# Attention: float16 maxima, one product per group, a new slot table, and the causal mask added by TensorE

## The reference, cut to what matters

```
scores = einsum('bhqd,bhkd->bhqk', q, k)        # 256 queries, 256 keys, per batch and head
scores = where(causal, scores, -inf)            # only in the self-attention of the third block
weights = softmax(scores, axis=-1)
out = einsum('bhqk,bhkd->bhqd', weights, v)
```

## Time and profile before

| | |
|---|---|
| Median of 3 runs | 3341.56 us (3337.22 to 3347.16) |
| The profiled execution, its own time | 3335.4 us |
| Its span, first to last instruction | 3333.7 us |
| Mean granted TensorE clock | 0.895 |
| PE busy | 2558.5 us (77%) |
| DVE busy | 2258.7 us (68%) |
| ACT busy | 1245.9 us (37%) |
| POOL busy | 924.7 us (28%) |

### The profile page before, as it was taken

The page is one execution under the profiler, slowest core; times in us unless marked ns, Lnnn a source line. Parts: engine busy times, 40 slices in busy tenths (PEclk is TensorE's granted clock), DMA queues, the critical chain, the costliest instruction groups (busy, mean ns, idle before and its releaser), DMA issues. The chain is left out here.

```text
span 3333.7 us, 58668 instructions
## 1 busy us (share of the span) xinstructions
PE 2558.5 (77%) x21348; PEld 1660.5 (50%) x21348; DVE 2258.7 (68%) x5909; ACT 1245.9 (37%) x2228; POOL 924.7 (28%) x1324
## 2 busy tenths in 40 slices
PE   2997367999424367997989776996799999869962
PEld 1443355666323135886456543443565555546651
DVE  5997745666467434666677777997666555777768
ACT  1886334333122103111346564772322222226611
POOL 3442460100350520112655325871000000024200
PEclk9998689999757678999989987998799999889986
DMA  4330454222322215665631012100100000011001
GB/s 111 114 130 30 161 203 154 76 76 77 114 80 80 76 39 181 221 226 192 215 101 52 17 48 93 47 22 5 61 9 12 1 1 1 6 38 46 21 8 56
DMA packets 158163, 266.84 MB, mean 80 GB/s; under 512 B 22635, under 2 KB 106137, under 8 KB 151876
## 3 DMA queue, kind: packets, MB, share of 16 engines
q1 hardware_dynamic: 131204, 186.97, 16.9%
q0 software_dynamic: 17904, 76.23, 6.8%
q10 hardware_dynamic: 8784, 0.04, 0.2%
HBM read 175.25 MB, written 88.34 MB: 79 GB/s over the span
## 5 line engine op out<-in xcount | busy, mean ns | idle before, releaser
L1380 ACT ACTIVATE l2e_hf<-l2e_H 128x512 f32<-128x512 f32 x208 | 124.2, 597 | 375.9 <-PE l2e_H L1336 375.9
L1416 DVE CAST l2e_hh<-l2e_hf 128x512 f16<-128x512 f32 x208 | 88.7, 427 | 127.1 <-ACT l2e_hf L1380 112.0
L688 DVE TENSOR_REDUCE l0a_mx<-l0a_S 128x2 f32<-128x512 f32 x256 | 164.3, 682 | 11.9 <-PE l0a_S L530 11.2
L1336 PE MATMUL l2e_H<-l2o_hi,l2e_w 128*128 128x512 f16 x576 | 151.8, 382 | 14.9 <-DVE l2e_w L1392 14.9
L637 ACT ACTIVATE l0a_pf<-l0a_ST 128x512 f32<-128x512 f32 x256 | 145.9, 598 | 40.5 <-PE l0a_ST L544 34.8
L228 POOL TENSOR_TENSOR l3in_n_rstd<-l3in_n_sq,all_mhalf 128x8 f32<-128x8 f32 x4 | 6.9, 1724 | 553.8 <-DVE l3in_n_sq L152 553.8
L1336 PE MATMUL l2e_H<-l2e_hh,l2e_w 128*128 128x512 f16 x640 | 155.1, 379 | 0.0
L684 DVE CUSTOM_DVE_ANT_0 l2s_masked<-l2s_S,l2s_mq 128x128 f32<-128x128 f32 (+1 forms) x512 | 150.7, 349 | 6.1 <-PE l2s_S L530 5.7
L1380 ACT ACTIVATE l0e_hf<-l0e_H 128x512 f32<-128x512 f32 x128 | 76.4, 597 | 206.7 <-PE l0e_H L1336 206.7
L1336 PE MATMUL l1e_H<-l1b_hi,l1e_w 128*128 128x256 f16 (+1 forms) x936 | 145.4, 275 | 7.8 <-DMA l1e_w<-packed,all_second_weight_row 7.8
L1418 DVE TENSOR_TENSOR l2e_hl<-l2e_hf,l2e_hh 128x512 f16<-128x512 f32 x208 | 144.0, 692 | 7.2
(11 more groups left out here) (726 smaller groups left out, 7448.6 us busy)
## 6 DMA issues: line engine op xcount, KB each, us to landing
l0e_wf<-in_L_ffn_w SPq DMA_DIRECT2D x16, 1024.0 KB, 7.2
rows<-l0a_zeros SPq DMA_DIRECT2D x16, 640.0 KB, 6.1
l1u_rb<-rows SPq DMA_DIRECT2D x20, 512.0 KB, 4.7
results<-l1e_y SPq DMA_DIRECT2D x39, 256.0 KB, 3.9
l0a_kv<-in_ctx SPq DMA_DIRECT2D x16, 512.0 KB, 4.3
rows<-l0a_zeros SPq DMA_DIRECT2D x16, 512.0 KB
l0d_p_cx<-in_ctx SPq DMA_DIRECT2D x16, 512.0 KB, 5.8
l0u_rb<-rows SPq DMA_DIRECT2D x16, 512.0 KB, 5.7
```

Of the source, the lines that this page charges most:

```text
L688: m = nc.vector.tensor_reduce(mx[h % 2][:, :, i], ps[:, :].rearrange("p (u k) -> p u k", u=TB), AX.X, ALU.max)
L1336: mm = pe.matmul(bank[0:fn, :], W[par][0:kn, at + k * wd + f0:at + k * wd + f0 + fn], X, start=(done == 0), stop=(done == k_all - 1))
L1380: nc.scalar.activation(hf[q % 4][0:fn, :], pair_of(q, lay)[0][0:fn, :], lay.func, scale=1.0 / WS).then_inc(acted, 1)
L1416: nc.vector.tensor_copy(high, v).then_inc(hi_done, 1)
```

## The change

It has five parts.

1. **Maxima in float16.** `mx` becomes float16, `bound` and `nm` are gone, and `turn_max` turns `mx` itself with the float16 identity. `copy_max` then copies float16 rows.
2. **One product per group in `divide`.** The two multiplications of 128x128 become one of 128x256; `on` gets another order of its elements, and GpSimd's `add` reads it accordingly.
3. **New slots.** With 16 heads `turn_max` moves from slot 1 to 2, `copy_max` and its DMAs from 3 to 4, `divide` from 4 to 3, and `turn` is split: queries at slot 5, keys at slot 7, both before at 4. With 8 heads `turn_back` moves from slot 2 to 1, `turn_max` from 0 to 1, `copy_max` from 1 to 2, `turn` from 2 to 3.
4. **Causal stage.** After each of the two `scoreT` products of a head TensorE adds the mask to the diagonal square: a product of the bfloat16 identity with `late` (0, or -2^100 where the key is later than the query), all 128 rows, 128 columns, into the same `ST`. `weigh` waits for `probs`.
5. `cut_late` is gone; GpSimd makes `late` and `ident_b` once, at the start of the stage.

```diff
-    BACK_AT, MAX_AT, TURN_AT = (1, 1, 4) if heads == 16 else (2, 0, 2)
-    COPY_AT, DIV_AT, KEYS_AT, SUM_AT = (3, 4, 1, 5) if heads == 16 else (1, 3, 1, 3)
+    BACK_AT, MAX_AT, TURN_Q_AT, TURN_K_AT = (1, 2, 5, 7) if heads == 16 else (1, 1, 3, 3)
+    COPY_AT, DIV_AT, KEYS_AT, SUM_AT = (4, 3, 1, 5) if heads == 16 else (2, 3, 1, 3)
...
-        mx = [st.sb(f"mx{i}", [P, TB, HALF]) for i in range(2)]
-        nm = [st.sb(f"nm{i}", [P, TB, HALF]) for i in range(2)]
+        mx = [st.sb(f"mx{i}", [P, TB, HALF], F16) for i in range(2)]
...
-                def cut_late(n):
-                    t = pf[n % NPF][:, 0:2 * S].rearrange("p (u q) -> p u q", u=TB)[:, :, 0:P]
-                    pool.wait_ge(probs, n + 1)
-                    nc.gpsimd.affine_select(out=t, in_=t, compare_op=ALU.is_ge, fill=0.0, base=0,
-                                            pattern=[[0, TB], [1, P]], channel_multiplier=-1).then_inc(cut, 1)
+                def make_late():
+                    nc.gpsimd.memset(late[:, :], 0.0).then_inc(late_set, 1)
+                    nc.gpsimd.tensor_copy(ident_b[:, :], g.ident[:, :]).then_inc(late_set, 1)
+                    pool.wait_ge(late_set, 2)
+                    nc.gpsimd.affine_select(out=late[:, :], in_=late[:, :], compare_op=ALU.is_ge, fill=NEG,
+                                            base=0, pattern=[[1, P]], channel_multiplier=-1
+                                            ).then_inc(late_set, 1)
...
                     m = pe.matmul(ST_ps[n % 2][:, t_at[u]:t_at[u] + S - query_from[u]],
                                   kT[h % RING][r0:r0 + rows, j, u * P:u * P + P],
-                                  qT[h % RING][r0:r0 + rows, j, query_from[u]:S], start=True, stop=True)
+                                  qT[h % RING][r0:r0 + rows, j, query_from[u]:S], start=True, stop=not causal)
+                    if causal:
+                        if n == 0:
+                            pe.wait_ge(late_set, 3)
+                        m = pe.matmul(ST_ps[n % 2][:, t_at[u]:t_at[u] + P], ident_b[:, :], late[:, :],
+                                      start=False, stop=True)
...
-                        pe.wait_ge(cut if causal else probs, (w + 1) * G)
+                        pe.wait_ge(probs, (w + 1) * G)
...
                 def turn_max(h):
-                    pe.wait_ge(nm_set, h + 1)
+                    pe.wait_ge(maxed, (h + 1) * HALF)
                     pe.wait_ge(q_turned, min(h + 3, NH))
                     for u in range(TB):
-                        m = pe.transpose(N_ps[0:HALF, u, :], nm[h % 2][:, u, :], g.ident[:, :])
+                        m = pe.transpose(N_ps[0:HALF, u, :], mx[h % 2][:, u, :], ident_h[:, :])
                     m.then_inc(nm_turned, 1)
...
-                def bound(h):
-                    dve.wait_ge(maxed, (h + 1) * HALF)
-                    if h >= 2:
-                        dve.wait_ge(nm_turned, h - 1)
-                    nc.vector.tensor_scalar(nm[h % 2][:, :, :], mx[h % 2][:, :, :], -NEG_H, NEG_H, ALU.min, ALU.max
-                                            ).then_inc(nm_set, 1)
```

More of the change, by code:

```diff
@@ L362, in attention_stage @@
         rs = st.sb("rs", [P, 2 * TB, G])
-        on = [st.sb(f"on{i}", [P, TB, P]) for i in range(2)]
+        on = [st.sb(f"on{i}", [P, 2, TB, P // 2]) for i in range(2)]
         ident_h = st.sb("ident_h", [P, P], F16)
@@ L513, in _ @@
                             make_mask()
+                            make_late()
                     if i == HALF - 1 and out_res is None and 0 <= j - 4 < NH:
@@ L565, in weigh, with turn, turn_queries @@
                         m.then_inc(weighed, 1)
-                def turn(h):
+                def turn(h, i):
+                    v = (qs, ks)[i][h // 2 % 2][:, :, :, :].rearrange("p t h r -> p t (h r)")
+                    for c in range(4):
+                        for u in range(TB):
+                            j = h % 2 * 4 + c
+                            m = pe.transpose(MH_ps[i][:, c * TB + u, :], v[:, u, j * P:j * P + P], ident_h[:, :])
+                    m.then_inc(chunks, 1)
+                def turn_queries(h):
                     b = h // 2
@@ L615, in _ @@
                         turn_max(j - 1)
-                    if i == TURN_AT and 0 <= j + 2 < NH:
-                        turn(j + 2)
+                    if i == TURN_Q_AT and 0 <= j + 2 < NH:
+                        turn_queries(j + 2)
+                    if i == TURN_K_AT and 0 <= j + 2 < NH:
+                        turn_keys(j + 2)
             @block.scalar
@@ L715, in divide @@
                         dve.wait_ge(o_done, h - 1)
-                    for u in range(TB):
-                        if out_res is None:
-                            dst = on[h % 2][:, u, :]
-                        else:
-                            dst = out_res[:, b * TB + u, h % 2 * P:h % 2 * P + P]
-                        m = nc.vector.tensor_tensor(
-                            dst.rearrange("p (s g d) -> p s g d", s=2, d=dh), sums[:, u:2 * TB:TB, :, 0:dh],
-                            rs[:, u:2 * TB:TB, :].unsqueeze(3).to_broadcast([P, 2, G, dh]), ALU.mult)
-                    m.then_inc(o_mul, 1)
+                    if out_res is None:
+                        dst = on[h % 2][:, :, :, :].rearrange("p s u (g d) -> p (s u) g d", d=dh)
+                    else:
+                        dst = out_res[:, b * TB:(b + 1) * TB, h % 2 * P:h % 2 * P + P].rearrange(
+                            "p u (s g d) -> p s u g d", s=2, d=dh)
+                        sums = sums.rearrange("p (s u) g e -> p s u g e", s=2)
+                    by = rs[:, :, :] if out_res is None else rs[:, :, :].rearrange("p (s u) g -> p s u g", s=2)
+                    nc.vector.tensor_tensor(
+                        dst, sums[..., 0:dh], by.unsqueeze(len(by.shape)).to_broadcast(list(by.shape) + [dh]),
+                        ALU.mult).then_inc(o_mul, 1)
                 for j, i, n in slots():
-                    if i == 0 and 0 <= j - 1 < NH:
-                        bound(j - 1)
                     if i == 0 and 0 <= j + 1 < NH:
```

26 lines of the change are left out of this document (11 added, 15 removed).

## The result

The changed kernel takes 3446.12 us (median of 4 runs, 3437.21 to 3464.36) against 3342.38 of the kernel before, a ratio of 1.0317 [1.0292, 1.0342]. That is +104 us where +76 was forecast: slower, as predicted, and 8 us above the upper end of the range. The profiled execution took 3439.64 us, span 3437.9, mean granted clock 0.888.

The account below looks back on a forecast made before the run. TensorE bounds the 8-head stages, VectorE l2s, both are near 89% busy in l0a; with masks TensorE bounds l2s. Causal +85, 8-head -16, l0a +7 make +76 on 3335.4, 3411, put at 3414 us; range 3362 to 3438.

Parts of the forecast that it names:

- The causal stage: In l2s, masks make TensorE set the round at 9.05 us, +2.6 us per round, +85 us in all.
- a switch, 0.09 us: On TensorE, each change of the array's form between products loses 0.09 us; a causal slot becomes 0.70 us.
- The weigh run ahead of `turn_max`: In the l2s round, two weigh runs are counted at 0.57 us each with a change of form behind them.
- half the switches: Rival for l2s: only the way back from each mask costs 0.09; stage +40 us, total about 3370; chance 0.10.
- the masks ride along: Rival for l2s: masks cost only their columns, round 6.5 us, total about 3308, faster; chance 0.06.
- The clock: Rival: l2s falls to 1.2 GHz, columns per round double, +150 us, total 3560; chance 0.03.
- The sum: All attention stages: +85 - 16 + 7 = +76 us on 3335.4 gives 3411 us; forecast put at 3414.
- The 8-head stages: l2a and l3a, bound by TensorE: round 5.75 to 5.46 us, -8 us per stage, -16 us together.
- The wait of 0.19 behind the weigh run: In l2a, turn_max waits 0.19 us for copy_queries; in slot 1 this wait goes.
- two float16 blocks instead of two float32 ones: turn_max gets cheaper, from 0.21 to 0.11 us, saving 0.10 per round in the 8-head stages.
- `l0a`: 16-head stage: new slots lengthen the round from 6.96 to 7.2 us, +7 us; range -12 to +13.
- the chain through `divide`, `copy_max` and the maxima of slot 4: In l0a, from S of slot 3 until score of slot 6 can start: 2.6 us of the 7.2 us round.

Follow-up runs that it names:

- experiment 3: Changed kernel with each 128-row mask product replaced by two 64-row products in the form of the neighbouring scoreT; ratio 1.005 to the kernel before.
- experiment 4: Changed kernel with each mask product issued twice in a row; one execution 3454.87 us, again 3454.01 us, ratio 1.0321 to the kernel before.
- Experiment 6: Changed kernel with turn_max widened to 128 columns in the 8-head stages; one execution, 3391.43 us, on the chip with 3265 us before.
- experiment 5: Changed kernel with the old slots in the 16-head stages; 3435.14 us, ratio 1.0273 to the kernel before.
- experiments 1: Changed kernel with its causal part undone, the mask back on GpSimd; ratio 0.9966 to the kernel before.
- the version of 8: Kernel before plus float16 maxima, single divide product, new 8-head slots and turn_max over 128 columns in all four stages; 3232.32 us against 3265.33, ratio 0.9895.
- experiment 7: Changed kernel again, 3389.09 us, ratio 1.0381; and with each turn transpose issued twice in the first eight halves of l2s, 3350.44 us, ratio 1.0256.

## Why the prediction was right or wrong

- **The causal stage: right in mechanism, and nearly so in size at the upper clock.** 84.5 to 89 us against 85. The switch is real, as experiments 3 and 4 show from both sides: no form changed, no switch; more products in one form, no further switch. The step "a switch, 0.09 us" was a little small: around the masks it is 0.105, which makes a slot 0.75 instead of 0.70 and a round 0.4 us longer. The weigh run ahead of `turn_max` takes 0.45 instead of 0.57, as no switch stands between the two, so the round is 9.30 instead of 9.05. Over 30 rounds that is 7 us more, and the first and last rounds give at least a part of it back. The Trainium skill ("TensorEngine Tiling (Array Packing)", Key Properties) lets a change of tiling mode drain the engine and a change of tile within a mode not; the trace agrees, with 0.105 us for the one and starts right behind the columns for the other. The rivals "half the switches" and "the masks ride along" fall with 0.16 us from mask to pair and a round of 9.30.
- **The clock: the step that failed.** The sum prices all 30 rounds of `l2s` at the upper clock and leaves the stretch at the lower one as it was, 32.7 us of the stage, at no cost and without a reason. The prediction knew of it ("a part of that stage ran at the lower level") but costed only a fall of the whole stage, at a chance of 0.03. "Nothing in the rows shows a fall while work follows work this closely" was true of the rows, and it was the wrong question: the stage begins at the lower level anyway, and what moved was the rise. The stretch, 41 us before, became 96 us here and between 72 and 198 in the other profiles of kernels with single masks of 128 rows. The term missing from the sum is 18 to 23 us; with it 3414 becomes 3432 to 3437, against 3446. For the profiled execution the rest of the 28 us between 3411 and 3440 is: the masks 0 to 4, the 8-head stages 4, `l0a` -5, and 7 between the stages. Why the rise comes later is open.
- **The 8-head stages: sign right, size off.** Forecast 5.46 us per round and -16, measured 5.63 and -12; of the 6 us per stage the rounds give 28 x 0.12 = 3.4, and the first reciprocal comes 2 us earlier. The wait of 0.19 behind the weigh run went, as said. The step that was mis-sized is "two float16 blocks instead of two float32 ones": 0.11. In the trace after, the turn of 4 float16 columns has a change of form of its own, on both sides:

```profile
1799.92 0.60 PE L610 MATMUL l2a_O<-all_ident,l2a_oT 128*128 128x128 f32 x4
1800.45 0.27 PE L603 MATMUL l2a_M<-l2a_ident_h,l2a_mx 128*4 128x128 f16 x2
1800.66 0.28 PE L531 MATMUL l2a_S<-l2a_kT,l2a_qT 128*128 128x256 f16 x1
```

  It takes 0.21 us to the next start, as did the float32 turn, and starts 0.20 behind the last block of `turn_back`, where blocks of one form follow 0.11 apart. Experiment 6 takes both away by widening it: 5.43.
- **`l0a`: right in mechanism.** Forecast 7.2, measured 7.15; the chain through `divide`, `copy_max` and the maxima of slot 4 can be read off VectorE's rows after:

```profile
152.37 0.70 DVE L702 TENSOR_REDUCE l0a_mx<-l0a_S 128x2 f16<-128x512 f32 x1 [0.29 <-PE l0a_S L531]
152.98 0.25 DVE L719 RECIPROCAL l0a_rs<-l0a_O 128x16 f32<-128x16 f32 x1
153.26 0.42 DVE L730 TENSOR_TENSOR l0a_on<-l0a_O,l0a_rs 128x256 f32<-128x256 f32 x1
153.61 0.27 DVE L710 COPY l0a_nmT<-l0a_M 8x256 f16<-8x256 f16 x1
153.80 1.87 DVE L702 TENSOR_REDUCE l0a_mx<-l0a_S 128x2 f16<-128x512 f32 x3
...
155.85 0.70 DVE L702 TENSOR_REDUCE l0a_mx<-l0a_S 128x2 f16<-128x512 f32 x1 [0.18 <-PE l0a_S L531]
```

  From the start of `S` of slot 3 (151.95) to that of slot 6 (154.54) it is 2.59 us, where the prediction had 2.6. A second path is as long within 0.03 us and was not in it: `turn` of the queries waits 0.45 us for `copy_max`, until 153.98, and `score` of slot 6 stands behind it. That the difference of 0.24 came out near 0.19 is in part luck, since the same working missed the round before by 0.23. The stage is only 2 us longer and not 7, since the first reciprocal comes 45.5 us into it instead of 49.5; `divide` one slot earlier, 0.9 us, explains only a part of that.

## What to carry to other kernels

Before an operation moves to TensorE, look at the part of the array that its neighbours use: if it needs another one, price a change on each side, per group of operations and not per operation, and ask whether it can be cut to the neighbours' form or stacked into one group. Count the time that a stage runs at the lower clock as a quantity that the change can move, and put it into the range. What an engine saves beside a chain that runs through another may come back as waits, as in experiment 5; follow the chain first.

## What the hardware showed that was not expected

- Around the start of `l2s` the lower clock of 1.2 GHz lasted 41 to 44 us in every profile of a kernel without changes of form around the masks (before, experiments 1 and 3, the version of 8), and 47.8 us in both with doubled masks. With single masks it lasted 95.6, 71.7, 75.1, 184.3 and 198.0 us. The two shortest of these are kernels with the old slots, and the two longest were taken on the chip with 3265 us before, so what sets the length among them is not shown. In these TensorE was busy 81 to 94% of the part that lies inside the stage. Repeated transposes brought the lasting rise from 173 to 50 us into the stage and 39 us off the total. Experiments 4 and 7 show that with more products it comes earlier; what the clock follows stays open.
- The spread of the changed kernel's time goes with the clock. Its mean granted clock, on record for every execution, goes 0.889, 0.888, 0.882, 0.876 in the order of the times 3437.21 to 3464.36, and 0.890, 0.888, 0.884, 0.881 in experiment 7. The runs with more products lie 4 to 5 us apart, with 0.891 to 0.892 (masks twice) and 0.903 to 0.906 (turned twice).
- The float16 turn of 4 or 8 columns has a form of its own beside full-width blocks (0.20 us behind a block of 128 columns instead of 0.11), while behind the float32 turn of the same 4 columns nothing was lost: its two blocks, 0.11 each, and the next product after 0.21 us. For 8 columns the float16 turn of experiment 5 shows it, 0.20 us behind the last block of `turn_back`; widening it as well brings `l0a` from 6.96 to 6.86 (experiment 8). Behind the weigh run in 32-column form it pays nothing (2205.41 + 0.45 = 2205.86) and pays the way to the pair instead.
- The type alone costs nothing there: in experiment 3 bfloat16 masks start 0.03 us apart amid float16 products in one 64-row form.
